# Stacks read by three transfers and a new order of the engines' work, in a four-block transformer kernel on one core

## The reference

```python
x = x + attn_a(layernorm(x)); x = x + ffn(layernorm(x))
x = x + attn_b(layernorm(x)); x = x + ffn(layernorm(x))

# attention a: 16 heads of 16, linear, causal, with 4 memories
sq, sk = elu(q) + 1, elu(k) + 1
num, den = sq . cumsum(sk v^T), clip(sq . cumsum(sk))
out = g * (memories read with sq, weighted by a softmax) + (1 - g) * num / den
# attention b: 16 heads of 16, rotary, causal softmax(q k^T / 4) v
# ffn: relu(x W1 + b1) W2 + b2, both weights quantized to -1, 0, 1
```

## Time and profile before

| | us |
|---|---|
| median of 3 runs | 2299.41 |
| lowest and highest | 2298.86, 2301.97 |
| the profiled execution | 2303.04 |
| its span, first to last instruction | 2301.3 |

### The profile page before, as it was taken

The page is one execution under the profiler, slowest core; times in us unless marked ns, Lnnn a source line. Parts: engine busy times, 40 slices in busy tenths (PEclk is TensorE's granted clock), DMA queues, the critical chain, the costliest instruction groups (busy, mean ns, idle before and its releaser), DMA issues. The chain is left out here.

```text
span 2301.3 us, 53268 instructions
## 1 busy us (share of the span) xinstructions
PE 1904.0 (83%) x18306; PEld 1207.5 (52%) x18306; DVE 1617.6 (70%) x3890; ACT 1361.3 (59%) x2694; POOL 1140.6 (50%) x978
## 2 busy tenths in 40 slices
PE   0447798989899898989889898989889898988786
PEld 0224455655555555555555555655555555555443
DVE  5546686968777786968777786968777786966351
ACT  0215375666667575666667575666667575665554
POOL 0236347364655547364655547364655547363322
PEclk9757799999999999999999999999999999999998
DMA  3101312304031322303032221304032221303020
GB/s 104 55 10 55 65 57 47 84 5 99 30 70 60 66 66 47 84 9 95 29 70 61 66 66 47 84 2 102 30 65 66 66 66 47 84 2 66 9 58 10
DMA packets 101756, 126.64 MB, mean 55 GB/s; under 512 B 19760, under 2 KB 88496, under 8 KB 97456
## 3 DMA queue, kind: packets, MB, share of 16 engines
q1 hardware_dynamic: 93104, 115.10, 19.8%
q10 hardware_dynamic: 8448, 8.39, 1.1%
HBM read 80.95 MB, written 42.47 MB: 54 GB/s over the span
## 5 line engine op out<-in xcount | busy, mean ns | idle before, releaser
L1268 DVE TENSOR_REDUCE mxs<-bank 128x1 f32<-128x128 f32 (+3 forms) x1024 | 428.0, 482 | 79.7 <-PE bank L1561 78.8
L907 ACT ACTIVATE place<-bank 128x512 f32<-128x512 f32 (+1 forms) x768 | 349.7, 532 | 104.4 <-PE bank L1575 103.1
L669 POOL TENSOR_TENSOR place<-am,place 128x512 f16<-128x512 f32 x256 | 291.0, 1157 | 203.2 <-ACT place L813 203.2
L659 POOL TENSOR_TENSOR place<-place 128x512 f16<-128x512 f32 x256 | 300.7, 1182 | 69.6 <-ACT place L801 64.0
L1559 PE MATMUL bank<-kst,qst 96*128 96x128 f16 (+3 forms) x1024 | 250.8, 306 | 33.5 <-DVE mxs L1268 16.9
L1420 PE MATMUL bank<-w2q,place 128*128 128x256 f16 x2048 | 248.2, 274 | 5.8 <-ACT place L798 4.2
L644 POOL TENSOR_TENSOR rstd<-ve,halfc 128x4 f32<-128x4 f32 x64 | 64.8, 1012 | 364.6 <-DVE ve L1043 364.6
L1573 PE MATMUL bank<-qst,kst 128*128 128x512 f16 (+3 forms) x1024 | 230.7, 302 | 14.6 <-DVE mxs L1268 6.5
L697 POOL TENSOR_TENSOR place<-place 128x512 f16<-128x512 f32 x64 | 83.1, 1301 | 280.9 <-ACT place L837 259.8
L1561 PE MATMUL bank<-mask_qk,identb 128*128 128x128 bf16 x1024 | 218.2, 222 | 0.0
L1420 PEld LDWEIGHTS bank<-w2q,place 128*128 128x128 f16 x2048 | 195.3, 98 | 40.8 <-ACT place L798 11.7
(11 more groups left out here) (162 smaller groups left out, 4134.9 us busy)
## 6 DMA issues: line engine op xcount, KB each, us to landing
by_head<-place SPq DMA_DIRECT2D x64, 256.0 KB, 2.3
qst<-by_head SPq DMA_DIRECT2D x256, 64.0 KB, 2.3
kst<-by_head SPq DMA_DIRECT2D x256, 64.0 KB, 2.3
by_dim<-place SPq DMA_DIRECT2D x64, 256.0 KB, 2.5
kst<-by_dim SPq DMA_DIRECT2D x64, 256.0 KB, 4.7
qst<-by_dim SPq DMA_DIRECT2D x128, 128.0 KB, 5.5
xa<-x SPq DMA_DIRECT2D x16, 512.0 KB, 4.0
out<-xg ACTq DMA_DIRECT2D x16, 512.0 KB, 3.4
```

The costliest lines, as they stand in the source:

```text
L659: G.tensor_tensor(L.hl[:, m, :], L.hf[:, m % 2, :], L.hh[:, m, :], ALU.subtract).then_inc(s["hl"], 1)
L669: G.tensor_tensor(alp[:, n % 2, k, :], am[:, k, :], ahp[:, n % 2, k, :], ALU.subtract).then_inc(s["al"], 1)
L907: A.activation(pf[h % SLOTS][:, S2_COL[k]:S2_COL[k] + S2_W[k]], bank_of(L2, ("S2", h, k))[:, 0:S2_W[k]], ACT.Exp, scale=D ** -0.5 / RS ** ...
L1268: V.tensor_reduce(mxs[:, g:g + 1], bank_of(L2, ("S1", n, k))[:, Q_AT[i]:Q_AT[i] + (i + 1) * P], AX, ALU.max).then_inc(s["mx"], 1)
```

## The change

Four things.

1. **Layout of the stacks.** The features of a half are no longer head by head in lane 1 but dimension by dimension (lane 2 had them by dimension already). In DRAM the bounce buffer is laid out with dimension first, then high and low, so that a stack's row is one contiguous run: 4 KB for lane 1 (4 heads), 8 KB for lane 2 (8 heads). The rows of a stack are now 4 x dimension + 2 x (part of q) + (part of k). Each half is then read by three transfers: one for `qst`, every DRAM row read into two neighbouring rows, and two for `kst`, with a step of two rows. Before, lane 1 used 16 transfers a half, lane 2 six. The bytes are the same.
2. **The bounce** is written by four transfers instead of two, each behind its own wait, so that the high half of q goes out before the low half of k is made.
3. **Setup.** The weights of lane 1's q and k are permuted when they are split (`split_by_dim`), and the mask for the states comes from a reduce of the identity instead of two selects on GpSimd. The chain on VectorE has 75 instructions.
4. **MARKS.** All marks are new, for every lane and engine; the steps are the same.

```diff
-LANDED = {1: 2 * 4 * 2 * 16, 2: 6 * 16}
+LANDED = {1: 3 * 16, 2: 3 * 16}
...
-                for part, src in enumerate((L.sth, L.stl)):
-                    to = by_head[half, part] if L is L1 else by_dim[half, :, part].rearrange("w p s -> p w s")
-                    sp.dma_start(to, src[:, 2 * half:2 * half + 2, :]).then_inc(s["bounced"], 16)
...
+                dims, rows = (by_row, P) if L is L1 else (by_dim, PARTS)
+                for which in range(2):
+                    at = 2 * half + which
+                    for part, (name, src) in enumerate((("sh", L.sth), ("sl", L.stl))):
+                        sp.wait_ge(s[name], due(L, name, t, at + 1))
+                        sp.dma_start(dims[half, which, :, part], src[:, at, :]).then_inc(s["bounced"], 16)
+
+                sp.wait_ge(s["bounced"], due(L, "bounced", t, 64 * (half + 1)))
+                stacks = L.qst.shape[1] // KH
+                of_half = slice(half * stacks, (half + 1) * stacks)
+                q_rows = dims[half, 0].rearrange("d a h s -> (d a) (h s)").rearrange("r (o f) -> r o f", o=1)
+                for part in range(2):
+                    k_rows = dims[half, 1, :, part].rearrange("(d o) h s -> d o (h s)", o=1)
+                    sp.dma_start(L.kst[part:rows:2, of_half, :].rearrange("p h s -> p (h s)"),
+                                 k_rows.broadcast_to([rows // 4, 2, stacks * S])).then_inc(L.landed[half], 16)
+                sp.dma_start(L.qst[0:rows, of_half, :].rearrange("p h s -> p (h s)"),
+                             q_rows.broadcast_to([rows // 2, 2, stacks * S])).then_inc(L.landed[half], 16)
...
+            def split_by_dim(mat):
+                stage = w_stage[mat // BQ][:, 0:2 * KH * H].rearrange("p (j i d) -> p j d i", i=QH, d=D)
+                hi, lo = (both(w, mat).rearrange("p (j d i) -> p j d i", i=QH, d=D) for w in (wh, wl))
+                for i in range(QH):
+                    link(V.tensor_scalar(hi[:, :, :, i], stage[:, :, :, i], WS, None, ALU.mult))
+                    link(V.scalar_tensor_tensor(lo[:, :, :, i], stage[:, :, :, i], WS, hi[:, :, :, i],
+                                                ALU.mult, ALU.subtract))
...
-            split_weights(0, BQ)
+            split_by_dim(AQ)
+            split_weights(AV, BQ - AV)
             split_by_parity(BQ)
...
+            link(V.tensor_reduce(bd4, ident[:, :].rearrange("p (j i) -> p i j", i=QH), AX, ALU.add))
```

Of the marks, those that the text below speaks of (lane 1, then lane 2, F2 and F1):

```diff
 # lane 1: sync
-            "PA": [61.6, 75.6],
+            "PA": [47.1, 90.6],
 # lane 1: dve
-            "NL": [82.7, 88.8, 98.4, 106.9, 113, 119.4, 127.5, 11.5, 18.4, 21.9],
+            "NL": [81.1, 87.3, 96.5, 104.2, 109.8, 116, 124.1, 12.8, 19.2, 21.8],
 # lane 1: pe
-            "N": [78.7, 83.4, 90.8, 98.8, 107.4, 113.5, 119.8, 0.1, 10.4, 18],
+            "N": [72.5, 82.9, 89.7, 97.5, 104.6, 110.2, 116.4, 0.1, 6.6, 16.9],
-            "NT": [81.6, 88, 97.5, 106, 112.1, 118.6, 126.6, 10, 17.5, 21],
+            "NT": [77.4, 88, 95.6, 103.3, 108.9, 115.2, 123.3, 6.5, 16.8, 19.7],
 # lane 2: sync
-            "PB": [18.1, 28.9],
-            "N": [45.3, 60.5, 74.5, 90.5],
+            "PB": [15.6, 28.1],
+            "N": [42.6, 56.8, 74.4, 89.4],
 # lane 2: pool
-            "PB": [11.3, 13.9, 17.4, 20.9],
+            "PB": [12.3, 14.9, 19.4, 22.5],
 # lane 2: act
-            "PB": [10.2, 11.9, 15.4, 17],
-            "PH": [14.9, 16.5, 24.9, 25.4],
+            "PB": [11.1, 13.7, 17.5, 19.1],
+            "PH": [14.9, 18.5, 27.5, 28],
 # lane 2: dve
-            "PL": [0, 15.6, 17.2, 25.6],
+            "PL": [0, 17.1, 20.6, 28.7],
 # lane 2: pe
-            "TT": [5.1],
-            "PB": [8.5, 10.3, 13, 14.4],
+            "TT": [4.4],
+            "PB": [8.3, 12.2, 14.6, 17.1],
-            "N": [30.3, 34.2, 35.3, 37.4, 42, 45.7, 48.8, 54.6, 59.1, 62.2, 67.3, 70.2, 72.9, 75.8, 81.5, 86],
+            "N": [30.3, 31.9, 32.7, 36.1, 38.2, 42.1, 49.1, 53.2, 55.5, 60.9, 65.5, 68.6, 72.8, 75.5, 80.5, 83.7],
-            "WO": [117, 120.1],
+            "WO": [111.4, 113.7],
 # F2: pool
-            "XB": [23.5],
+            "XB": [9.5],
 # F2: act
-            "FT": [12.9],
+            "FT": [7.3],
 # F2: pe
-            "FTT": [15.8],
-            "UP": [21.4, 22.3, 23.3, 27.1, 28, 29, 31.1, 32.1],
+            "FTT": [10.9],
+            "UP": [15.9, 20.1, 21.2, 22.4, 27.2, 31, 33.8, 34.7],
```

More of the change, by code:

```diff
@@ L474, in build @@
         primed = sem("primed")
-        DVE_SETUP = 66
+        DVE_SETUP = 75
         block = ctx.enter_context(nc.Block())
@@ L519, in _ @@
                 for h in range(HH8):
-                    sp.dma_start(bm[h * D:(h + 1) * D, half, :, h % QH, :], mem[half * HH8 + h]).then_inc(m_in, 16)
+                    r, i = divmod(h, QH)
+                    sp.dma_start(bm[r * PARTS + i:(r + 1) * PARTS:QH, half, :, i, :],
+                                 mem[half * HH8 + h]).then_inc(m_in, 16)
             sp.wait_ge(primed, 1)
@@ L537, in stack @@
-                heads = slice(half * HH8, (half + 1) * HH8)
-                pairs = slice(half * HH8 // 2, (half + 1) * HH8 // 2)
-                if L is L2:
-                    for k in range(2):
-                        sp.dma_start(L.kst[2 * k * D:2 * (k + 1) * D, heads, :].rearrange("p h s -> p (h s)"),
-                                     by_dim[half, 1].rearrange("a (d h) s -> (a d) (h s)", h=HH8)
-                                     ).then_inc(L.landed[half], 16)
-                        for j in range(2):
-                            row = (2 * k + j) * D
-                            sp.dma_start(L.qst[row:row + D, heads, :].rearrange("p h s -> p (h s)"),
-                                         by_dim[half, 0, k].rearrange("(d h) s -> d (h s)", h=HH8)
-                                         ).then_inc(L.landed[half], 16)
-                    return
@@ L550, in stack @@
-                for k, (q_part, k_part) in enumerate(((0, 0), (0, 1), (1, 0), (1, 1))):
-                    for dst, part, which in ((L.qst, q_part, 0), (L.kst, k_part, 1)):
-                        rows = by_head[half, part, :, which, :]
-                        for r in range(2):
-                            to = slice(r * PARTS + k * D, r * PARTS + (k + 1) * D)
-                            sp.dma_start(dst[to, pairs, :], rows.rearrange("(g r d) s -> r d g s", r=2, d=D)[r]
-                                         ).then_inc(L.landed[half], 16)
+                dims, rows = (by_row, P) if L is L1 else (by_dim, PARTS)
@@ L623, in _ @@
                             pattern=[[1, P]], channel_multiplier=-1).then_inc(pool_const, 1)
-            G.affine_select(out=bd8, in_=bd8, compare_op=ALU.is_ge, fill=0.0, base=0,
-                            pattern=[[-D, HH8]], channel_multiplier=1).then_inc(pool_const, 1)
-            pool.wait_ge(pool_const, 13)
-            G.affine_select(out=bd8, in_=bd8, compare_op=ALU.is_ge, fill=0.0,
-                            base=D - 1, pattern=[[D, HH8]], channel_multiplier=-1).then_inc(pool_const, 1)
             pool.wait_ge(c_in, 96)
-            pool.wait_ge(pool_const, 14)
+            pool.wait_ge(pool_const, 11)
             for L in (L1, L2, F2, F1):
@@ L1026, in _ @@
                                    bm[rows, :, :, :, D].rearrange("p a m h -> p (a m) h")))
-                link(V.tensor_copy(bdmask[rows, :, :], bd8[rows, heads].rearrange("p (h o) -> p h o", o=1)
+                link(V.tensor_copy(bdmask[rows, :, :], bd4[rows, :].rearrange("p (h o) -> p h o", o=1)
                                    .broadcast_to([PARTS, QH, VW])))
```

159 lines of the change are left out of this document (76 added, 83 removed), and 36 rows, old and new, of the table MARKS.

## The result

The changed kernel takes 2382.48 us (median of 4 runs, 2369.32 to 2387.3) beside 2300.69 us for the kernel before on the same chip: a ratio of 1.0344, interval 1.0325 to 1.0362. It is 3.4% slower where the forecast was 2.2% faster.

A forecast was written before the change was run, and what follows sets the result against it. No engine is full; PE, busiest at 83%, idles on waits. Thirteen turns at -3.5 (-45.5), pieces around the loop -2.7, before the loop -1.5: -49.7 us; 2303.0 - 49.7 - 3.6 (profiled run above median) = 2249.7 us, range 2222 to 2291.

The forecast's parts named there:

- What bounds the kernel, and what a turn is worth: No engine is full over a loop turn of 129.57 us; one cost per turn counts 13 times.
- Setup, +2.0 us: VectorE's chain before the loop: permuting lane 1's q and k weights and one reduce add 2.0 us (+0.5 to +6.3).
- First turn's stack, -3.5: In the first turn, which runs alone, PE's 3.46 us wait for the stack goes whole; at worst 1.4 us stays.
- The pieces around the loop: Straight code before and after the loop carries parts of the same lists and gains 2.7 us in all.
- Lane 1's stacks at 0 in the loop: Fewer transfers for lane 1's stacks gain nothing in the loop, being hidden beside lane 2's heads.
- Part A: Turn's start up to PE's first scores of lane 2: 32.1 us instead of 33.1, a gain of 1.0 a turn.
- the rival that was slower through this add: F2's late normed tile makes GpSimd's bias add stall lane 2's rotation and first scores: 2311 us, chance 0.14.
- the range of 6.3 to 7.7: Lane 2's stack, first read to last landing, in us: 6.3 if issue bounds it, 7.7 if transfer does; 7.0 taken.
- Part B, -2.6 us a turn, from the marks' span: First scores of lane 2 to the turn's end: 94.1 us by the new marks against 96.7, PE idle 2.7.
- the rival of the small gain: PE's waits close up in another place, so only 1.0 us a turn is gained: 2285 us, chance 0.18.
- the wrong sign "a wait of PE for lane 2's stack of over 1 us in each turn": PE waiting over 1 us for `qst<-by_dim` in each turn would show the forecast wrong.
- The sign of a turn of 129 us with A shorter and B longer: A 129 us turn, shorter before lane 2's first scores and longer after them, would show the forecast wrong.

The follow-up runs named there:

- e11: Kernel before's order with the new stacks and 120 one-element VectorE memsets ahead of the loop, under the wait for weights: 2302.39 us, ratio 0.9999.
- e9: Kernel after with 120 one-element VectorE memsets ahead of the loop, under the wait for weights: 2348.85 us, ratio 1.0187.
- e4: Kernel before with its own stacks, only the table MARKS replaced by the new one: 2388.73 us, ratio 1.0371.
- e17: e9 with lane 2's first scores one up projection later and lane 1's GpSimd bias add behind lane 1's first gate product: 2296.41 us, ratio 0.9982.
- e12: New stacks and 120 memsets as in e11; new marks up to 41 us of the turn, old marks behind: 2304.68 us, ratio 1.0005.
- e15: e12 with lane 2's first scores one up projection later: 2295.05 us, ratio 0.9968.
- e18: e11 with only GpSimd's bias add of lane 1 moved behind lane 1's first gate product: 2279.05 us, ratio 0.9898.
- e16: e15 with GpSimd's bias add of lane 1 moved behind lane 1's first gate product: 2275.21 us, ratio 0.9883.
- e1: Kernel before with nine one-element VectorE memsets more ahead of the loop: 2332.24 us, ratio 1.0123.
- e2: Kernel after with twenty one-element VectorE memsets more ahead of the loop: 2365.41 us, ratio 1.0272.
- e5: Kernel after with 119 one-element VectorE memsets ahead of the loop, under the wait for weights: 2394.69 us, ratio 1.0401.
- e10: e9 with lane 2's first scores two up projections later and lane 1's bias add behind its second state product: 2357.21 us, ratio 1.0237.
- e13: New stacks and 120 memsets as in e11; new marks up to 79.5 us of the turn, old marks behind: 2361.71 us, ratio 1.0263.

## Why the prediction was wrong

- **What bounds the kernel, and what a turn is worth**: right. The loss is 13 times a loss per turn, and it shows in the starts of `xb`.
- **Setup, +2.0 us**: right. The first statistics of `xa` are at 66.2 us before and 68.3 after. **First turn's stack, -3.5**: the wait of 3.46 us is gone; PE's next wait there is 0.77 us for VectorE. Yet the first `xb` starts at 239.80 against 239.73, so the sum up to there was 0.1, and at the start of the loop it is +3.4 (369.35 against 365.96), not -1.5 us. The pieces around the loop were put at -2.7; the sum's own shares, half and a third of 3.5, give -2.9.
- **Lane 1's stacks at 0 in the loop**: right in the old order (e11).
- **Part A**: nearly right in its time, 32.5 us for 32.1, and in its steps:

```profile
1198.60 2.34 POOL L638 TENSOR_TENSOR xg<-xg,b2bc 128x1024 f32<-128x1024 f32 x1 [1.24 <-ACT place L749]
1201.68 1.27 POOL L704 TENSOR_TENSOR place<-place,sint 128x512 f32<-128x512 f32 x1 [0.73 <-ACT place L863]
...
1205.04 5.28 SPq L537 DMA_DIRECT2D by_dim<-place  x4
1212.07 1.19 SPq L545 DMA_DIRECT2D kst<-by_dim  x2
1213.30 0.59 SPq L547 DMA_DIRECT2D qst<-by_dim  x1
...
1221.08 0.23 PE L1552 MATMUL bank<-kst,qst 96*128 96x128 f16 x1 [2.93 <-DMA qst<-by_dim]
```

The bias add of F2 ends 12.3 us into the turn (forecast 12.7) and the first rotation starts at 13.1 (the sign of a late one was 13.5). So the rival that was slower through this add did not come about. The reads start at 23.5 us (22.9 to 24.0) but take 8.9 us to the last landing, above the range of 6.3 to 7.7: the single transfer of 512 KB took 7.7 us here, though the median has less (the row above it is lane 1's transfer of the same size, into all 128 partitions):

```profile
qst<-by_row SPq DMA_DIRECT2D x32, 512.0 KB, 4.8
...
qst<-by_dim SPq DMA_DIRECT2D x32, 512.0 KB, 6.4
```

That term was mis-sized at its start. It put the median of the earlier trace rows, 5.5 us, behind the last issue of the kernel before. There the last of the six takes 6.7 us and the reads 8.9 in all (mean of 11 turns), not 7.7. What fewer issues take off was nearly right: the reads take 7.5 us in e11 against 8.9 in the old order, 8.8 in e9 against 9.6 (e4) in the new one.
- **Part B, -2.6 us a turn, from the marks' span**: this is the step that failed. The forecast priced the new order by its own table (94.1 us), and e9's part B, without any gap at the branch, takes 100.1 us:

```profile
1202.46:1302.60 100.14, 92.94 (x963) 60.06 (x963) 75.81 (x189) 63.95 (x129) 47.59 (x42) 0.98 0.18 53
```

That the old table matched the trace within 0.8 us in B was taken as a warrant for the new one. But the marks give an order and planned times, and no hold of VectorE by GpSimd is in them. Where the old order had the add beside `nt`, the new one put it beside `winv`, ahead of the maxima that PE needs. The text followed the bias add of F2 with care and never asked what F1's does to VectorE. And even without that hold (e17), the new order is worth 0.2% against the kernel before and not 2%: its part B takes 97.6 us (mean of 13 turns; 96.4 in the kernel before), and PE idles 6.3 us in it, where the forecast had 2.7. The waits of the earlier trace rows did not halve, they went to other places, as the rival of the small gain had said; which order would bring 94.1 us stays open.
- **The signs**: the wrong sign "a wait of PE for lane 2's stack of over 1 us in each turn" is what the trace shows (43.4 us in 16 turns). Its effect is small with these stacks: e12 has the same wait and 2305 us, e15 without most of it 10 us less. The sign of a turn of 129 us with A shorter and B longer came in its second half: A is shorter, B longer, and the turn 136 us.
- **Missing altogether**: that nine more instructions of setup move the loop's code. The forecast priced them at 2 us. They cost 34 us more.

In sum, of 2382 us 34 are the code fetches (e9) and 52 the place of the add together with the later scores (e17); what is left, 2296 us, is the change with these mended, level with or 0.2% under the kernel before. That the kernel after came out slower had a chance of 0.14 in the forecast, but through another add and another wait.

## What to carry to other kernels

Before a schedule is judged, look whether the start of a loop pass has an "issue" gap and whether the queue for code moves packets inside the loop; if so, shift the loop by some instructions under an idle stretch and measure again. Here shifts of 20 and 119 left the fetches in, and one of 120 ended them. A table of planned times prices no interference between engines: for every long GpSimd instruction that moves, read which VectorE instructions with two SBUF inputs will run beside it, and who waits for them. The best kernel of this study is the old order with the new stacks and one mark moved, 2279 us (e18), or 2275 us with the new first part and later scores (e16), whose difference the intervals do not settle.

## What the runs showed of the hardware

- A VectorE loop body of 376 or 377 recorded instructions ran without fetches at one place against the 128-instruction pieces and fetched five pieces a pass at three others, for 2.6 to 5.3 us at each branch (before, e9, e11; after, e1, e2, e5).
- A VectorE instruction of 0.18 us with two inputs in SBUF took 2.2 us beside a GpSimd add of 2.34 us (e11), and one of 0.19 us took 2.4 (e9), once in each of the 13 turns. The maxima, with their input in PSUM, took their usual 1.68 us beside such an add (e10).
- At waits of PE of about 1.9 to 3 us the granted clock went to half for 3.4 us (e9 above), so that such a wait can cost nearly twice its length. It did not do so at each: it stands at the stack's wait in 10 of 13 turns of e12, and at the wait for the maxima in 12 of 13 turns of e9 but 3 of e13.
- Why e13 is 13 us slower than e9, which has more of the new order, stays open. Its trace has both holds, `winv` for 2.4 us and one `nt` for 1.08 in each turn, and PE waits 0.5 us a turn for `nt` where e9 has no such wait; that is half of the 1.0 us between their turns.
